# Cross sums in DRAM by batch, position and head: row stores on all DMA engines, and sixteen small loads in place of one

## What is computed

```
def step(S, inp):
    qt, kt, vt, at, bt = inp
    err = jnp.einsum('bhij,bhj->bhi', S, kt) - vt
    S = at[..., None] * S - bt[..., None, None] * (err[..., None] * kt[:, :, None, :])
    o = jnp.einsum('bhij,bhj->bhi', S, qt)
    return (S, o)
_, o = lax.scan(step, S0, xs)        # 512 positions
```

## Time and profile before

| what | us |
|---|---|
| median of 3 runs (lowest, highest) | 7076.88 (7072.87, 7079.59) |
| the profiled execution, its time | 7082.73 |
| its span, from the first to the last instruction | 7080.9 |
| recurrence with the start, to about | 4212 |
| the rest (end of layer 0, layer 1), about | 2870 |
| DVE busy, of the span | 5420.1 |
| POOL busy, of the span | 3639.8 |

### The profile page before, as it was taken

How to read it: one execution, slowest core, us unless ns; L and a number is a source line. 1 busy time by engine, 2 the same in 40 slices (tenths; PEclk the granted TensorE clock), 3 DMA queues, 4 the chain that set the end, 5 groups by cost and what they waited for, 6 DMA issues and landing times. The chain is left out here.

```text
span 7080.9 us, 176655 instructions
## 1 busy us (share of the span) xinstructions
PE 5011.9 (71%) x58695; PEld 3311.0 (47%) x58695; DVE 5420.1 (77%) x15973; ACT 3320.2 (47%) x7234; POOL 3639.8 (51%) x4232
## 2 busy tenths in 40 slices
PE   5666766666667666667666626888888888888877
PEld 4555555455555555555555523344444444444433
DVE  5889888888898888888888855666666666666665
ACT  4554455445544554455444513444444444444444
POOL 3778777877787778787877761111111111111110
PEclk8877777787777778787777757888888888888888
DMA  4666666666666666666666641111111111111111
GB/s 121 164 159 163 168 164 155 168 167 165 155 168 169 160 158 167 167 167 157 164 168 159 161 123 42 45 45 45 48 45 45 45 45 45 45 45 45 47 45 36
DMA packets 1197390, 804.68 MB, mean 114 GB/s; under 512 B 1049827, under 2 KB 1101699, under 8 KB 1188484
## 3 DMA queue, kind: packets, MB, share of 16 engines
q1 hardware_dynamic: 1134212, 610.21, 36.1%
q10 hardware_dynamic: 62464, 185.09, 8.2%
HBM read 490.57 MB, written 304.55 MB: 112 GB/s over the span
## 5 line engine op out<-in xcount | busy, mean ns | idle before, releaser
L469 POOL TENSOR_TENSOR qp<-qp,ab 128x512 f32<-128x512 f32 (+7 forms) x1024 | 980.0, 957 | 75.3
L474 POOL TENSOR_TENSOR qp<-qp,pt 128x512 f32<-128x512 f32 (+7 forms) x1024 | 961.6, 939 | 80.2
L1778 DVE TENSOR_REDUCE nmax<-w_bank 128x1 f32<-128x512 f32 x1024 | 643.0, 684 | 405.7 <-PE w_bank L1360 401.3
L851 DVE SCALAR_TENSOR_TENSOR p_bank<-y,conv_w,p_bank 128x128 f32<-128x128 f32 x3072 | 825.5, 347 | 50.7 <-ACT p_bank L668 22.8
L1315 POOL TENSOR_TENSOR ot<-ot,ln_w 128x1024 f32<-128x1024 f32 x64 | 150.7, 2355 | 1143.2 <-ACT ot L1617 1143.2
L535 PE MATMUL d_bank<-st 64*32 64x80 f32 x16384 | 493.5, 289 | 340.6 <-issue 315.0
L471 POOL TENSOR_TENSOR pt<-qp,vb 128x512 f32<-128x512 f32 (+7 forms) x1024 | 724.3, 707 | 11.4 <-DVE vb L928 9.3
L507 PE MATMUL d_bank<-xd,kt 32*64 32x128 f32 x7936 | 354.7, 328 | 455.9 <-DVE st L869 392.1
L1320 POOL TENSOR_TENSOR x1b<-x,bias 128x256 f32<-128x256 f32 x64 | 46.3, 723 | 1165.7 <-DVE bst L1874 1165.7
L599 PEld LDWEIGHTS p_bank<-xnT,wqkv 128*128 128x128 f32 x4096 | 548.4, 216 | 187.6 <-issue 187.6
L599 PE MATMUL p_bank<-xnT,wqkv 128*128 128x128 f32 x4096 | 597.1, 306 | 43.1 <-ACT st L681 34.9
(11 more groups left out here) (219 smaller groups left out, 11656.1 us busy)
## 6 DMA issues: line engine op xcount, KB each, us to landing
db<-decay_dram SPq DMA_DIRECT2D x124, 1024.0 KB, 12.3
prod_dram<-prod ACTq DMA_DIRECT2D x128, 640.0 KB, 7.9
kp<-prod_dram SPq DMA_DIRECT2D x512, 80.0 KB, 2.6
qp<-prod_dram SPq DMA_DIRECT2D x256, 160.0 KB, 2.9
a_dram<-at ACTq DMA_DIRECT2D x64, 512.0 KB
ab<-a_dram SPq DMA_DIRECT2D x64, 512.0 KB, 5.8
v_dram<-vt ACTq DMA_DIRECT2D x64, 512.0 KB
vb<-v_dram SPq DMA_DIRECT2D x64, 512.0 KB, 5.7
```

Source lines behind the costliest of these rows:

```text
L469: link(nc.gpsimd.tensor_tensor(q, q, ab[:, g, r:r + 1, :].to_broadcast([128, w, DV]), ALU.mult), 1)
L474: link(nc.gpsimd.tensor_tensor(q, q, pt2[:, 0:w], ALU.add))
L851: nc.vector.scalar_tensor_tensor(out=zz, in0=y[:, j % Y_BANKS, i, :, tap:tap + C], scalar=conv_w[:, m, tap:tap + 1], in1=zz, op0=ALU.mult, ...
L1778: nc.vector.tensor_reduce(nmax[:, n:n + 1], bank[:], AX.X, ALU.max, negate=True).then_inc(freed, 1)
```

## The change

The DRAM buffer of the cross sums is laid out by sequence, position and head, in place of position, sequence and head. In it the rows of `xo` are whole rows in the same order, so each store is one pattern of 128 rows of 2 KB; before, it was a pattern of 8 sequences by 16 positions by 2 KB. In the new buffer sequence and head are no longer one step apart, so the load is cut by sequence: eight loads of rows 0 to 7 (16 partitions by 8 rows of 256 bytes, 32 KB), then eight of rows 8 to 15. The first eight raise `xk_in`, on which DVE waits; the last eight raise a new semaphore `xq_in`, on which POOL waits.

```diff
-    x_dram = [dram(f"x_dram{g}", [C, GB, H, DV]) for g in range(GROUPS)]
+    x_dram = [dram(f"x_dram{g}", [GB, C, H, DV]) for g in range(GROUPS)]
...
 (SP)
                     sp.wait_ge(*dma_of(x_wr, n, g, 0, 32))
                     held(sp, sp_passed)
-                    sp.dma_start(xk[:], x_dram[g].rearrange("t b h i -> (b h) t i")).then_inc(xk_in[g], 16)
+                    for landed, rows in ((xk_in[g], slice(0, HALF)), (xq_in[g], slice(HALF, C))):
+                        for b in range(GB):
+                            sp.dma_start(xk[H * b:H * b + H, rows], x_dram[g][b, rows].rearrange("t h i -> h t i")).then_inc(landed, 16)
...
 (POOL)
-                        pool.wait_ge(*dma_of(xk_in, n, g, 0))
+                        pool.wait_ge(*dma_of(xq_in, n, g, 0, 16 * GB))
...
 (ACT)
                 if due(dma_of(xk_in, n, g, -2)[1]):
-                    act.wait_ge(*dma_of(xk_in, n, g, -2))
+                    act.wait_ge(*dma_of(xk_in, n, g, -2, 16 * GB))
+                    act.wait_ge(*dma_of(xq_in, n, g, -2, 16 * GB))
...
-                    dst = x_dram[g][:, :, HP * u:HP * u + HP].rearrange("t b h i -> b t (h i)")
+                    dst = x_dram[g].rearrange("b t h i -> (b t) (h i)")[:, 512 * u:512 * u + 512]
                     act.dma_start(dst, xo[:, 512 * u:512 * u + 512]).then_inc(x_wr[g], 16)
...
 (DVE)
-                    dve.wait_ge(*dma_of(xk_in, n, g, 0))
+                    dve.wait_ge(*dma_of(xk_in, n, g, 0, 16 * GB))
```

More of the change, by code:

```diff
@@ L259, in layer0_recurrence @@
         values_scaled, cross_done = sem("values_scaled"), sem("cross_done")
-        e_wr, xe_in, x_wr, xk_in = ([sem(f"{name}{g}") for g in range(GROUPS)] for name in ("e_wr", "xe_in", "x_wr", "xk_in"))
+        e_wr, xe_in, x_wr, xk_in, xq_in = ([sem(f"{name}{g}") for g in range(GROUPS)] for name in ("e_wr", "xe_in", "x_wr", "xk_in", "xq_in"))
         kl_in = [sem(f"kl_in{g}") for g in range(GROUPS)]
```

## The result

| what | before | changed |
|---|---|---|
| median of 4 runs (lowest, highest), us | 7075.85 (7072.87, 7079.59) | 7314.66 (7285.82, 7341.18) |
| ratio, 95% interval | | 1.034 (1.030 to 1.038) |
| span of the profiled execution, us | 7080.9 | 7307.7 |

What follows compares the result with a forecast made beforehand. DVE, busy 77%, was taken as the bound, with its wait for `xk`; after the change POOL's chain rules. Gain 1.05 us a slot x 56 = 59 us: 7082.73 to 7024, less 6 for the median: 7018; range 6985 to 7060 (53%).

Steps and rivals of the forecast that it cites:

- The stores: Second store of the sums to first load: 2.8 us in place of 5.19, bounds 2.4 and 3.7, using 16 engines.
- The sign named for it: If the stores' step was right, the DMA share would be near 1 while the sums are stored.
- The issue of the loads: SP's sixteen loads: 0.48 us each, bounds 0.40 and 0.65; sixteen issues in 7.7 us.
- The pieces are small and issued slowly, so the queue never fills: Argument against contention of the sixteen loads with the 512 KB `a_dram` store still on the move when they start.
- The key rows: DVE's rows of `xk` are there 6.4 us after the first issue, against 7.25 and 7.55 before.
- POOL's query rows come eight issues later: 6.4 + 8 x 0.48, rounded up to 10.3 us.: POOL's rows land 10.3 us after the first issue, against 7.3 and 7.6 before; bounds 9.1 and 12.9.
- rival 4: Slower: POOL's chain is longer, from 0.56 us an issue or query rows at 11.4 us; to 7160; 18% with the fixed-cost rival.
- L912, POOL's chain, the wait at the copy: L912 at 0.63 us, POOL's chain rules, DVE waits about 1 us at L911 and 3 to 4 at L918.
- What is moved past: SP's later issues slip 7.2 us less 2.4; decays' transfers move 1 to 2 us; `kp` keeps some 4 us of cover.
- Its first cause: Issues of 0.65 us on SP, as for `kp`: 1.5 us a slot, 84 us, to 7160.
- Its second, contention: The 512 KB `a_dram` store, still on the move when the loads start, could also make POOL's chain the longer one.
- Rival 5: Each of the sixteen loads pays a fixed cost of over 2 us: over 20 us a slot, beyond 8100; 2%.

Runs made afterwards that it cites:

- e1: The changed kernel with ACT's store to `v_dram` moved behind the first product store: 7128.88 us, 1.006 of the kernel before.
- e11: The changed kernel with the `v_dram` store cut: 64 of 1024 columns at the old place, 960 behind the first product store: 7141.90 us, 1.009 of before.
- e12: The changed kernel with the `a_dram` and `beta_dram` stores moved behind the last SiLU, right ahead of `v_dram`'s: 7461.30 us, 1.055 of before.
- e6: The kernel before, its one load of `xk` cut into two (rows 0 to 7 for DVE, 8 to 15 for POOL), old stores: 7038.93 us, 0.995.
- e7: The changed kernel with a row of padding behind each sequence in `x_dram`, so the stores stay 8 by 16 rows: 7454.81 us, 1.055 of before.
- e9: The kernel before with only ACT's stores to `a_dram` and `beta_dram` moved behind the last SiLU: 6971.03 us, 0.987 of before.

## Why the prediction was wrong, point by point

- **The stores**: right in kind, 0.5 us too high. From the second store to the first load 2.3 us, 0.1 below the lower bound of 2.4. The sign named for it came true as well. The 128 rows of the second store move between 1630.85 and 1631.55 us, and in these 0.7 us ACT's queue takes nearly all of the 16 engines (a window of 2 us around it has a share of 0.46 and hides this):

```profile
q10 hardware_dynamic: 130, 0.25, 97.2%
```

- **The issue of the loads**: the price was right, its evenness not. Issue and landing of all pieces in the tile view of `xk`, beside the earlier trace rows:

```profile
L353 SPq DMA_DIRECT2D xk<-x_dram x1024: 320/431/2566, 139.3 to 4425.4; - x171
...
L915 DVE TENSOR_TENSOR rows_bank<-kp,xk x64: 624/628/634, 146.1 to 4423.7; 128x448 f32<-128x448 f32 x64
...
DMA to landing us min/median/max: 1.8/2.2/7.8
```

  0.43 us and 0.04 of gap make 0.47, where 0.48 was forecast. But single issues take up to 2.57 us, the second one about 2 us in most slots, next to `a_dram`, and a late one after `v_dram` goes out. From first to last it is 9.2 us and not 7.2. "The pieces are small and issued slowly, so the queue never fills" was false in what matters: issues do stall.

- **The key rows**: 7.2 us after the first issue, 6.4 forecast. The stretched second issue is in front of all of them.

- **The step that failed: "POOL's query rows come eight issues later: 6.4 + 8 x 0.48, rounded up to 10.3 us."** They come after 15.5 us. In the three slots without a large store inside the series it is 9.2, 1.1 less than forecast. The term has no part for what ACT's queue stores while the series runs, and there are two such stores: `v_dram`, issued 7 to 8 us after the first load, costs 4.0 us (15.46 against e1's 11.48), and `a_dram`, which mostly goes out 1.7 us ahead of the first load, about 2.2 us (11.48 against 9.24). The first was left out; the second was named under rival 4 and dismissed. The kernel before has the store to `v_dram` at about the same place, in the slot of the earlier trace rows ahead of DVE's use of the rows at 1562.27:

```profile
1560.07 0.59 ACTq L704 DMA_DIRECT2D v_dram<-vt  x1
```

  It does no harm there: POOL has its rows 7.6 us after the issue in the mean of the 36 slots (of 8 to 55) in which the store goes out less than 6.5 us after the load's issue, and 7.7 us in that of the 12 others. The issue of the single load is over after 0.35 us, ahead of the store; in the series the last pieces are issued only when the store is there too. I had read from the trace of before which stores run beside the load, found `a_dram`, and not asked what is issued up to 10 us after it. With 5.2 us more on this term and 0.5 less on the stores, the forecast of 63.4 us a slot becomes 68.1, where 68.0 was measured.

- **L912, POOL's chain, the wait at the copy**: right in kind. L915 takes 0.63 us; L468 to the end of L418 takes 23.2 us (23.4 forecast); DVE waits 1.6 us at its rows (about 1 forecast) and, at the copy, 6.8 us and not 3 to 4 for the instruction named.

- **What is moved past**: right for `kp`. At the copy, of 448.6 us of idle time 443.2 are POOL's and 5.4 the loads' of `kp`:

```profile
L921 DVE COPY rows_bank<-kp 128x448 f32<-128x448 f32 x64 | 40.2, 627 | 448.6 <-POOL vb L418 443.2 <-DMA kp<-prod_dram 5.4
```

- **The rivals.** Rival 4 stated that slower begins when the query rows land 11.4 us after the first issue. No run tests that threshold: e1 and e11, with 11.5 and 11.7, are 0.6% and 0.9% slower than before, but by the changed kernel's own terms the slot would be as long as before only at 64.43 - 26.83 - 2.31 - 23.24 - 0.14 = 11.91 us, and both are slower because of the 0.9 to 1 us that they lose ahead of the stores. Its first cause (0.65 us an issue) did not occur. Its second, contention, did: by the store that it named for 2.2 us, and for 4.0 by one that it did not name. Its price of 84 us was that of the first cause, so the direction was among the rivals, at 18%, and its size was not. Rival 5 fell: the landing of one piece is 2.2 us in the median, and it overlaps with the next. Still, of the same 512 KB, sixteen loads of 32 KB make the slot longer than eight of 64 KB (68.0 against 64.1 us). The Trainium skill, DMA: Bandwidth & Descriptors, rules for kernel authors, says to coalesce transfers under 64 KB; the runs agree with the advice. The overhead per piece, the reason that it gives, explains 15 x 0.47 = 7 us of the series and not the further 6.2 that the two stores cost.

**How a store of large rows delays small pieces.** In the first six microseconds of the series, and then in the eight from `v_dram`'s issue on, the DMA view of the same slot shows:

```profile
q10 hardware_dynamic: 268, 0.48, 33.0%
q1 hardware_dynamic: 984, 0.22, 17.1%
```
```profile
q1 hardware_dynamic: 785, 0.91, 48.8%
q10 hardware_dynamic: 136, 0.52, 27.2%
```

In the second window, 8 us long, ACT's packets are 0.52 MB / 136 = 3.8 KB each in the mean, and one takes 0.272 x 16 x 8 / 136 = 0.26 us. A piece of `xk` has 128 rows of 256 bytes, 8 for each engine if they are spread over all 16. The Trainium skill, DMA: Bandwidth & Descriptors, section on queues, rings and completion order, says that each DMA engine takes turns between queues and finishes a whole packet of some 9 to 17 descriptors before it switches. If the store has 16 rows on each of 8 engines, that would be, as an estimate, a turn of up to 16 x 0.26 = 4.1 us in which a piece stands still; the last piece lands about 7 us after its issue where others take 2, so 5 more. The size fits, but the trace shows more than such turns could do. The last piece is issued at 1640.98 us. From 1642.62 to 1644.30 the DMA view has

```profile
q10 hardware_dynamic: 48, 0.20, 44.9%
q1 hardware_dynamic: 6, 0.00, 0.2%
```

So for 1.7 us ACT's store takes the time of 7 of the 16 engines (44.9% of 16), SP's queue next to none on any engine, though a load of decays is issued behind the piece, and about half of the engines' time is idle. The last 128 of the 2048 packets of `xk`, a whole piece, start after this stretch. At the start of the series it is the same: 64 packets of 256 bytes move, which is half a piece, and then none for 1.85 us, while `a_dram`'s store takes 48.2% (1633.65 to 1635.05 us). A pause of 1 us or more between packets 1001 and 1990 of `xk`'s 2048 is in 30 of the 48 slots of the changed kernel, in 47 of e12's and in none of e1's and e11's. Turns on the engines that the store uses would leave the other half of a piece free to move; something holds SP's queue as a whole, and what it is stays open. What is shown: what the store moves decides (e11), its place relative to the series decides (e1, e12), and its issue as such does not.

## What to carry to other kernels

When one transfer is cut into a series, its price is the landing of the last piece, and the series covers a stretch of time in which other queues issue their own transfers: list what each queue issues in that stretch, with its bytes and the size of its rows, before adding up issue times. A waiting engine's load is worth keeping clear of large stores from another queue; moving one such store (and a small one) from 4.2 us ahead of the load to 2.7 behind it, 7.5 us later in the slot, made the kernel before 1.3% faster, with no other edit. A store that is issued shortly ahead of the series counts too, not only those inside it. And cut for the reader that needs its part first (two loads, 0.5% faster, e6), not finer than the layout forces.

## What was not expected of the hardware

- Beside a store of 512 KB from ACT's queue single issues on SP's queue take up to 2.57 us in place of 0.43, and a piece of 32 KB lands up to 7.8 us after its issue in place of 2.2.
- While such a store holds 7 to 8 of the 16 engines, SP's queue can stand still on all of them, for 1.7 us in the slot shown.
- The same store with a sixteenth of its bytes, in rows of 256 bytes, does nothing of the kind (11.7 against 15.5 us for the query rows).
- Two such stores close together cost more than one by one: 18.2 us, and a series of issues of 12.3 us in place of 9.2.
- Written as 128 rows, the two stores of the sums let the load start after 2.3 us, as 8 by 16 rows after 4.9 to 5.0, with the same bytes (e7).
- One load of 2048 rows of 256 bytes takes 4.9 us alone and 7.6 beside the store (e9); from that store it loses 2.7 us, where the last of sixteen small ones loses 4.0 from the store to `v_dram` alone and 6.2 from both.
